# One macaron block on one core: second router's scores inside the latent attention, VectorE's output addition ahead of the row sums, the dense attention's small steps placed anew, expert lists and gathers earlier

## The chip, the core and the metric

The kernel runs on one core of one Trainium2 chip. The time is that of one launch on the device, in microseconds (us). Engines are named as in the profile: PE is TensorE's matrix multiply and PEld its weight load, DVE is VectorE, ACT is ScalarE, POOL is GpSimd, SP is SyncE, which here only issues DMAs. Lines (L554) are those of the kernel before, except where the text says that they are the changed kernel's.

## What is computed

x has 16 sequences of 512 tokens with 128 channels: 8,192 tokens, which lie as 64 tiles of 128 tokens (one batch is 4 tiles). Six residual steps follow one another, each on the layer norm of the current x:

```python
x = x + 0.5 * routed_ffn(ln(x))        # f1
x = x + latent_attention(ln(x))        # la, causal, 16 heads of 8
x = x + 0.5 * routed_ffn(ln(x))        # f2, same weights as f1
x = x + 0.5 * experts(ln(x))           # m1
x = x + cosine_attention(ln(x))        # ca ("dense"), 16 heads of 8, biases
x = x + 0.5 * experts(ln(x))           # m2
```

The routed step adds two attentions over its input. The light one works in windows of 128 tokens with 8 heads of 64. The heavy one works on 128 query and 256 key tokens per sequence, which a router picks: a score `x . routing_token` per token (one routing token for queries, one for keys), 50 steps of a coordinate descent over the 512 scores of each of 32 rows, and the largest. The expert step computes a shared feed-forward for all tokens, and routes tokens to 64 experts with a capacity of 48 rows each: their rows are gathered, multiplied and added back by scatter.

## The kernel before

`macaron_block` (L2332) runs the stages in order, each with its own arena in the on-chip memory and its own `Block`, at whose end all engines meet. x and y, the tokens before and after a stage, stay on chip. Within a block every engine has its program written out by hand, and the engines meet through counting semaphores; the order on an engine, and on SP's and POOL's DMA queues, is the order in the code.

**Router (`router_prologue`, L81).** It loads and scales the light weights (`wqkv`, `wo` in `lw`), takes the statistics of all 64 tiles (L226, DVE), and computes the scores on PE: per batch four transposes (L172), a split of the transposed tile into a bf16 part on ACT (L205) and a rest on DVE (L219), and four products (L181, L183). Then variance, square root on ACT (L209), reciprocal, a transpose of the reciprocals (L192), and scores (L254) and their maxima (L256) as 48 rows of 512. It runs twice, as f1r and f2r.

**Light attention (`light_attention`, L259).** One `body` per window of 128 tokens, 64 windows. In one window DVE takes the maxima of the logits (L534), subtracts them (L538), makes a step of the descent (`settle` L528, `descend` L522 and L523), sums the probabilities that ACT made (L546), takes the reciprocal (L550), adds the output of window i-3 to x (L554) and normalises the next tile (`make_xr`, L513). POOL multiplies the probabilities by the reciprocals (L371, two operations a window). PE's transpose of the next tile (L425) and the output of L407 share the PSUM tile `ps_a`, so PE waits at L425 for L554, and DVE waits at L513 for L425. The descent ends after window 27; from 28 on DVE carries the search for the largest scores instead, and ACT makes the next tile.

**Latent and dense attention (`stacked_attention`, L997).** Both treat 16 batches; one batch is 4 quads. The latent one has 10 units in a quad, the dense one 4 units of 4 heads in each, 16 places in a batch. The logits are computed twice from operands in bf16 parts: once for the maxima (L1302, then DVE L1721 or L1719), once with the maxima subtracted (L1313, then ACT's exponential L1575). The maxima go through a split in two bf16 parts (`mparts`), a transpose (L1382), a copy (L1742) and four small DMAs into the operand (`m_rows`, L1171). Queries and keys of a later batch are split by POOL into parts (L1187 to L1199), stored to HBM (L1151) and loaded as stacks (L1163), all on SP's queue. In the latent attention POOL also masks probabilities (L1202) and splits the maxima (L1210, L1212); in the dense one DVE splits them (`split`, L1730 and L1732). The output (L1413) is added to y by DVE: one addition in the latent attention (L1761), bias and then y in the dense one (L1763, L1765), and there `tile_stats` (L976) takes the statistics for the next stage.

**Experts (`moe_block`, L1852).** For each batch k, PE and ACT compute the shared part, POOL adds x to it (L2045) and SP stores it (L1998). After the last of these stores SP writes the list of expert tokens (L2000) and reads it back to all partitions (L2002), and POOL, after the last addition, issues the first six gathers (L2030). Then gathers, the experts' products (from L2142) and scatters (L2062) follow in a chain.

## Time and profile before

| | us |
|---|---|
| median of 3 runs (lowest to highest) | 3302.72 (3302.44 to 3307.93) |
| the profiled execution's own time | 3303.23 |
| its span | 3301.5 |
| PE busy | 2797.7 (85%) |
| DVE busy | 2312.4 (70%) |
| ACT busy | 1849.4 (56%) |
| POOL busy | 1476.8 (45%) |

| stage, by the instructions' names | from, us | to, us |
|---|---|---|
| router and light attention of f1 | 0 | 530 |
| heavy attention of f1 | 530 | 785 |
| latent attention | 785 | 1544.7 |
| router of f2 | 1544.7 | 1590.6 |
| light attention of f2 | 1590.6 | 2095 |
| heavy attention of f2 | 2095 | 2350 |
| experts m1 | 2350 | 2600 |
| dense attention | 2600 | 3062 |
| experts m2 | 3062 | 3301.5 |

The stages follow one another with a meeting of all engines between them, so what a stage gains or loses goes into the span one for one. The busy shares are averages over stages of different kinds. The profile's chain that ended last reaches back only through m2 (DMA 3%, PE 3% of the span), so each stage is read from its own stretch of the timeline and of the waits.

### The profile page before, as it was taken

The page shows a single profiled execution, that of the slowest core. Times are in us where ns is not written, and L with a number is a line of the kernel's source. Part 1 is how long each engine was busy: PE and PEld are TensorE (multiplying, and loading weights), DVE is VectorE, ACT ScalarE, POOL GpSimd, SP SyncE. Part 2 cuts the span into 40 slices and gives each one's busy share as a digit, 9 for nine tenths or more (in the row PEclk, how much of TensorE's full clock was granted, in tenths as well). Part 3 has the DMA queues.
Part 4 walks back from the last instruction along what each step waited for, and adds up shares of the span by engine and source line. Part 5 has one row for each costly group of instructions (what it writes and reads, how often), then busy time and mean ns, then how long its engine had stood idle before and what let it go on. Part 6 is the DMA issues. An engine that isn't in the chain of part 4 may idle for free. (4 is left out here: it accounts for less than half of the span.)

```text
span 3301.5 us, 72698 instructions
## 1 busy us (share of the span) xinstructions
PE 2797.7 (85%) x24552; PEld 1869.8 (57%) x24552; DVE 2312.4 (70%) x6126; ACT 1849.4 (56%) x3771; POOL 1476.8 (45%) x1662
## 2 busy tenths in 40 slices
PE   7999998997699999998888999799785278887774
PEld 4777886775233333333567777677663145555642
DVE  5887776884588888883677777599662267786641
ACT  3777664553166666664577666455541257776421
POOL 1222236883455555542122223578555354451445
PEclk9999998998599999998999999899895579999775
DMA  2000000001333333320000000000162255553532
GB/s 80 1 0 1 0 0 1 0 0 31 77 78 79 79 79 81 87 68 14 14 0 0 1 0 0 1 0 0 50 164 35 82 138 124 135 127 88 142 86 31
DMA packets 158029, 162.92 MB, mean 49 GB/s; under 512 B 43264, under 2 KB 136064, under 8 KB 157056
## 3 DMA queue, kind: packets, MB, share of 16 engines
q1 hardware_dynamic: 148032, 148.24, 17.5%
q0 software_dynamic: 9216, 7.87, 1.8%
q10 hardware_dynamic: 576, 4.19, 0.3%
q8 instruction: 114, 1.87, 0.2%
q14 instruction: 91, 0.75, 0.1%
HBM read 84.57 MB, written 74.60 MB: 48 GB/s over the span
## 5 line engine op out<-in xcount | busy, mean ns | idle before, releaser
L1721 DVE CUSTOM_DVE_ANT_0 la_ps<-la_ps,la_tri 128x512 f32<-128x512 f32 (+3 forms) x1024 | 480.4, 514 | 91.9 <-PE la_ps L1302 84.2
L1575 ACT ACTIVATE la_prob<-la_ps 128x512 f32<-128x512 f32 x640 | 374.0, 601 | 236.0 <-PE la_ps L1313 229.1
L371 POOL TENSOR_TENSOR f2l_prob<-f2l_prob,f2l_rec 128x512 f32<-128x512 f32 x128 | 132.2, 1054 | 364.2 <-DVE f2l_rec L550 364.2
L1202 POOL TENSOR_SCALAR_AFFINE_SELECT la_prob<-la_prob 128x512 f32<-128x512 f32 x256 | 159.4, 635 | 298.9 <-ACT la_prob L1575 298.7
L1302 PE MATMUL la_ps<-la_ks,la_qs 48*128 48x512 bf16 (+3 forms) x1024 | 255.3, 318 | 42.2 <-DVE la_mx L1721 26.9
L371 POOL TENSOR_TENSOR f1l_prob<-f1l_prob,f1l_rec 128x512 f32<-128x512 f32 x128 | 133.9, 1067 | 334.2 <-DVE f1l_rec L550 334.2
L1313 PE MATMUL la_ps<-la_qs,la_ks 50*128 50x512 bf16 (+3 forms) x1024 | 243.0, 311 | 4.4 <-ACT la_prob L1575 1.8
L1313 PEld LDWEIGHTS la_ps<-la_qs,la_ks 50*128 50x128 bf16 x1024 | 67.2, 94 | 234.3 <-ACT la_prob L1575 170.8
L1345 PE MATMUL la_ps_o<-la_prob,la_v 128*32 128x512 f32 (+3 forms) x2048 | 196.0, 456 | 0.0
L1719 DVE TENSOR_REDUCE ca_mx<-ca_ps 128x4 f32<-128x512 f32 x256 | 163.7, 680 | 39.8 <-PE ca_ps L1302 39.5
L1575 ACT ACTIVATE ca_prob<-ca_ps 128x512 f32<-128x512 f32 x256 | 140.4, 598 | 38.1 <-PE ca_ps L1313 36.2
L1721 DVE DVE_READ_ACCUMULATOR2_ANT la_mx<- 128x1 f32 x1024 | 142.8, 139 | 0.0
L400 PE MATMUL f1l_ps_qk<-f1l_xrT,f_wqkv 128*128 128x128 f32 x1024 | 134.5, 286 | 0.7 <-ACT f1l_xrT L496 0.7
L400 PE MATMUL f2l_ps_qk<-f2l_xrT,f_wqkv 128*128 128x128 f32 x1024 | 134.1, 285 | 0.7 <-ACT f2l_xrT L496 0.7
L1302 PEld LDWEIGHTS la_ps<-la_ks,la_qs 48*128 48x128 bf16 x1024 | 67.0, 95 | 110.6 <-DVE la_mx L1721 89.9
L400 PEld LDWEIGHTS f1l_ps_qk<-f1l_xrT,f_wqkv 128*128 128x128 f32 x1024 | 122.1, 195 | 11.7 <-issue 10.4
L400 PEld LDWEIGHTS f2l_ps_qk<-f2l_xrT,f_wqkv 128*128 128x128 f32 x1024 | 121.8, 195 | 11.8 <-issue 10.6
L1313 PE MATMUL ca_ps<-ca_qs,ca_ks 58*128 58x128 bf16 x1024 | 91.9, 224 | 41.2 <-DMA ca_ks<-stack_image 15.3
L1313 PEld LDWEIGHTS ca_ps<-ca_qs,ca_ks 58*128 58x128 bf16 x1024 | 61.1, 97 | 103.1 <-issue 60.7
L1187 POOL TENSOR_TENSOR ca_rr<-ca_qb,ca_t 128x512 f32<-128x512 f32 x32 | 44.1, 1379 | 164.9 <-ACT ca_t L1644 164.9
L546 DVE TENSOR_REDUCE f2l_rsum<-f2l_prob 128x8 f32<-128x1024 f32 x64 | 78.1, 1220 | 55.8 <-ACT f2l_prob L479 55.8
L546 DVE TENSOR_REDUCE f1l_rsum<-f1l_prob 128x8 f32<-128x1024 f32 x64 | 78.1, 1220 | 54.5 <-ACT f1l_prob L479 54.5
(551 smaller groups left out, 7979.2 us busy)
## 6 DMA issues: line engine op xcount, KB each, us to landing
stack_image<-la_parts SPq DMA_DIRECT2D x192, 128.0 KB, 2.4
stack_image<-ca_parts SPq DMA_DIRECT2D x192, 128.0 KB, 2.3
la_qs<-stack_image SPq DMA_DIRECT2D x64, 192.0 KB, 3.5
la_ks<-stack_image SPq DMA_DIRECT2D x64, 192.0 KB, 4.4
ca_qs<-stack_image SPq DMA_DIRECT2D x64, 192.0 KB, 3.8
ca_ks<-stack_image SPq DMA_DIRECT2D x64, 192.0 KB, 4.8
gather_table<-m_xn SPq DMA_DIRECT2D x32, 256.0 KB, 2.3
gather_table<-m_pr SPq DMA_DIRECT2D x32, 128.0 KB, 2.3
```

The lines of the kernel that those rows point to most:

```text
L371: nc.gpsimd.tensor_tensor(pr[:, g], pr[:, g], rc[:, g].rearrange("p (h o) -> p h o", o=1).broadcast_to([P, PAIRS, P]), ALU.mult).then_inc( ...
L400: last = nc.tensor.matmul(ps_qk[:, t, p], wqkv[:, t, p * P:(p + 1) * P], xrT[:], start=True, stop=True)
L546: nc.vector.tensor_reduce(rsum[:], prob[(u - 1) % 2][:], X_AX, ALU.add).then_inc(sum_ready, 1)
L1187: nc.gpsimd.tensor_tensor(rr[:], left[:], right[:], op)
L1202: return nc.gpsimd.affine_select(view, view, pattern=[[0, 4], [1, P]], compare_op=ALU.is_ge, fill=0.0, base=0, channel_multiplier=-1)
L1302: last = nc.tensor.matmul(bank[:, col:col + width], qs[u][rows, h // 2, qblk * P:(qblk + 1) * P], ks[u][rows, h // 2, keys], start=True, s ...
L1313: last = nc.tensor.matmul(bank[:, col:col + width], ks[u][rows, h // 2, blk * P:(blk + 1) * P], qs[u][rows, h // 2, blk * P:blk * P + widt ...
L1345: last = nc.tensor.matmul(ps_o[32 * j:32 * j + 32, blk * P:T], v[u][:, blk, 4 * q + j, :], prob[q % 2][:, unit, col:col + width], start=bl ...
L1575: nc.scalar.activation(prob[q % 2][:, n], ps2[n % 2][:], ACT.Exp, scale=SM).then_inc(S["p_sb"], 1)
L1719: last = nc.vector.tensor_reduce(m, bank[:].rearrange("p (a b) -> p a b", a=TPB), X_AX, ALU.max)
L1721: last = nc.vector.tensor_tensor_reduce(bank[:, col:col + width], bank[:, col:col + width], tri[:, T - width:T], 1.0, -BIG, ALU.add, ALU.m ...
```

## The change

1. **Router of f2.** Its 64 tiles' scores and statistics are computed while the latent attention runs. POOL multiplies the finished tiles of batch i-2 with the two centred routing tokens and adds the products up in halves (`route_dots`, three parts between the masks of quad 1); those of the last batch follow after its output. DVE takes the four statistics of batch i-1 among the maxima of quad 3. A short `router_end` takes the place of `router_prologue` for f2. The light weights stay on chip from f1.
2. **Light attention, f1 and f2.** L554, the addition of the output of window i-3, moves ahead of the wait for ACT's probabilities.
3. **Dense attention.** The small steps of a batch are placed at 16 places instead of 8 slots, on PE, DVE and ACT. POOL splits the maxima (casts before L1730 on DVE) and adds the output bias to y; DVE adds the output once. SP stores the first half of batch i+3's parts (t = 0) one body earlier and loads the first half of the stacks before the rows of maxima.
4. **Experts, m1 and m2.** The token list is stored before the output of k = 12 and read back before that of k = 13, and POOL issues the first six gathers in pairs after its additions k = 13, 14 and 15.

The heavy attention and the router of f1 are as before.

```diff
@@ router_end, vector
+            ch.step(nc.vector.tensor_tensor(diff[:], col(1), col(4), ALU.subtract))
+            nc.vector.tensor_tensor(ssq[:], col(2), col(5), ALU.add)
+            ch.step(nc.vector.tensor_tensor(diff[:], diff[:], diff[:], ALU.mult))
+            nc.vector.scalar_tensor_tensor(ssq[:], diff[:], C / 4.0, ssq[:], ALU.mult, ALU.add).then_inc(ssq_ready, 1)
+            dve.wait_ge(ssq_ready, 1)
+            nc.vector.tensor_scalar(var[:], ssq[:], 1.0 / C, LN_EPS, ALU.mult, ALU.add).then_inc(var_ready, 1)
...
+            dve.wait_ge(std_ready, 1)
+            nc.vector.reciprocal(rstd[:], std[:]).then_inc(rstd_ready, 1)
...
+            nc.vector.tensor_tensor(wide[:, :, 0:B], by_batch(dots[:, 0]), by_batch(rstd[:]), ALU.mult)
+            nc.vector.tensor_tensor(wide[:, :, KV0:KV0 + B], by_batch(dots[:, 1]), by_batch(rstd[:]), ALU.mult).then_inc(wide_ready, 1)
...
+            dve.wait_ge(r_ps, 1)
+            nc.vector.tensor_copy(s_rows[:], ps_r[:]).then_inc(rows_ready, 1)
+            nc.vector.tensor_reduce(smax[:], ps_r[:], X_AX, ALU.max)
@@ light_attention, vector, body
+                if live(i, 3):
+                    dve.wait_ge(f_ps, i - 2)
+                    j = i - 3
+                    nc.vector.scalar_tensor_tensor(
+                        y[:, bass.ds(j, 1), :].rearrange("p o c -> p (o c)"), ps_a[:, 2], 0.5,
+                        x[:, bass.ds(j, 1), :].rearrange("p o c -> p (o c)"), ALU.mult, ALU.add).then_inc(y_ready, 1)
                 if live(i, 1):
                     dve.wait_ge(p_sb, i)
                     nc.vector.tensor_reduce(rsum[:], prob[(u - 1) % 2][:], X_AX, ALU.add).then_inc(sum_ready, 1)
@@ stacked_attention, gpsimd
+            def route_dots(b, part):
...
+                    for r in range(2):
+                        last = nc.gpsimd.tensor_tensor(prod[:, r], ys, rtok[:, r:r + 1].broadcast_to([P, TPB, C]), ALU.mult)
...
+                for k, half in ((1, 64), (2, 32)) if part == 1 else ((3, 16), (4, 8), (5, 4), (6, 2), (7, 1)):
...
+                    nc.gpsimd.tensor_tensor(to, low, high, ALU.add).then_inc(S["dot_step"], 1)
             def body(i, u):
+                if not latent:
+                    if live(i):
+                        split_maxima(i, 1)
+                    if live(i, -2):
+                        split(i + 2, 1, 2, 5)
+                    if live(i, -1):
+                        split_maxima(i + 1, 0)
+                    if live(i):
+                        add_bias(i)
+                    if live(i, -3):
+                        split(i + 3, 0, 0, 5)
+                        split(i + 3, 1, 0, 2)
+                    return
...
+                if i == B:
+                    for part in range(3):
+                        route_dots(B - 1, part)
@@ stacked_attention, vector, between
+                if live(i, 1) and q == 3 and n in STATS_AT:
+                    dve.wait_ge(S["out_done"], i)
+                    nc.vector.nop(nofuse=True)
+                    j = TPB * (i - 1) + STATS_AT[n]
+                    nc.vector.bn_stats(stats[:, j], y[:, j])
@@ moe_block, sync
+                if k == LISTED - 1:
+                    sp.wait_ge(S["left_ready"], 1)
+                    sp.dma_start(lists.rearrange("(e s) -> e s", e=E), left[:].rearrange("e a s -> e (a s)")).then_inc(S["lists_stored"], 16)
+                if k == LISTED:
+                    sp.wait_ge(S["lists_stored"], 16)
+                    sp.dma_start(tb, lists.rearrange("(a s) -> a s", a=1).broadcast_to([P, E * CAP])).then_inc(S["tb_in"], 16)
```

DVE, light attention of f2, the descent, first before, then changed (`g_x` is the stage's output, `g_y` its input, `f2l_xr` the next tile normalised):

```order
L523 TENSOR_SCALAR f2l_tmin<-f_s_rows,f_na 48x512
L545 ISA
L546 TENSOR_REDUCE f2l_rsum<-f2l_prob 128x8
L547 ISA
L549 ISA
L550 RECIPROCAL f2l_rec<-f2l_rsum 128x8
L552 ISA
L554 ISA x2
L554 SCALAR_TENSOR_TENSOR g_x<-f2l_ps_a,g_y 128x128
L558 ISA
L513 ISA x2
L513 REGISTER_ALU
```

```order
L590 TENSOR_SCALAR f2l_tmin<-f_s_rows,f_na 48x512
L612 ISA
L614 ISA x2
L614 SCALAR_TENSOR_TENSOR g_x<-f2l_ps_a,g_y 128x128
L618 ISA
L619 TENSOR_REDUCE f2l_rsum<-f2l_prob 128x8
L620 ISA
L622 ISA
L623 RECIPROCAL f2l_rec<-f2l_rsum 128x8
L625 ISA
L580 ISA x2
L580 REGISTER_ALU
```

The addition (L554, now L614) stands ahead of the row sums, and the normalising of the next tile (L513, now L580) directly behind the reciprocal.

POOL, latent attention, quads 1 and 2 of a batch of the changed kernel (L1286 is the mask, `la_prod` the products, `fw_dots` the finished sums, L1295 and L1298 the split of the maxima):

```order
L1286 AFFINE_SELECT la_prob<-la_prob 128x4x128 x2
L1334 TENSOR_TENSOR la_prod<-g_y,la_rtok 128x512 x2
L1286 AFFINE_SELECT la_prob<-la_prob 128x4x128 x2
L1344 TENSOR_TENSOR la_prod<-la_prod 128x8x64
L1344 TENSOR_TENSOR la_prod<-la_prod 128x8x32
L1286 AFFINE_SELECT la_prob<-la_prob 128x4x128
L1344 TENSOR_TENSOR la_prod<-la_prod 128x8x16
L1344 TENSOR_TENSOR la_prod<-la_prod 128x8x8
L1344 TENSOR_TENSOR la_prod<-la_prod 128x8x4
L1344 TENSOR_TENSOR la_prod<-la_prod 128x8x2
L1344 TENSOR_TENSOR fw_dots<-la_prod 128x2x4
L1295 CAST la_mparts<-la_mx 128x32
```

Nine operations of the router stand between the masks and ahead of the split of the maxima; before, the masks and the split stood alone there.

POOL, dense attention, one batch of the changed kernel (`g_y` with `ca_bo` is the bias), in which the two splits of the maxima and the bias stand among the splits of queries and keys that were alone on POOL before:

```order
L1278 TENSOR_TENSOR ca_r<-ca_rr,ca_parts 128x512
L1280 TENSOR_TENSOR ca_parts<-ca_rr,ca_parts 128x512
L1283 TENSOR_TENSOR ca_parts<-ca_r,ca_parts 128x512
L1295 CAST ca_mparts<-ca_mx 128x32
L1298 TENSOR_TENSOR ca_mparts<-ca_mx,ca_mparts 128x32
L1321 TENSOR_TENSOR g_y<-g_y,ca_bo 128x512
L1271 TENSOR_TENSOR ca_rr<-ca_qb,ca_t_0 128x512
L1275 TENSOR_TENSOR ca_parts<-ca_qb,ca_t_0 128x512
L1278 TENSOR_TENSOR ca_r<-ca_rr,ca_parts 128x512
L1280 TENSOR_TENSOR ca_parts<-ca_rr,ca_parts 128x512
L1283 TENSOR_TENSOR ca_parts<-ca_r,ca_parts 128x512
```

The rest of the batch (the operations for the keys and the other split) repeats this pattern; the split of the maxima waits for the maxima that it reads, and what stands behind it waits too.

## Rows read from the trace of the kernel before

**Rows 1.** Windows, dense attention: us; busy PE, PEld, DVE, ACT, POOL; clock; DMA share; GB/s
```profile
2720.00:2960.00 240.00, 198.50 (x2938) 134.94 (x2936) 186.44 (x378) 174.02 (x331) 117.83 (x96) 0.98 0.52 131
```

**Rows 2.** Timeline (start us, us, instruction, idle before), latent attention to second light attention
```profile
1543.05 0.69 DVE L1761 TENSOR_TENSOR g_y<-la_ps_c,g_y 128x512 f32<-128x512 f32 x1 [2.58 <-PE la_ps_c L1413]
...
1581.65 0.26 DVE L232 TENSOR_TENSOR f2r_total<-f2r_st 128x64 f32<-128x64 f32 x1
...
1583.55 0.58 ACT L207 COPY f2r_dots<-f2r_ps_d 48x512 f32<-48x512 f32 x1 [2.54 <-PE f2r_ps_d L183]
1584.15 1.28 ACT L209 ACT_TABLE_LOAD   x1
...
1588.81 0.68 DVE L256 TENSOR_REDUCE f_smax<-f_s_rows 48x1 f32<-48x512 f32 x1
...
1590.62 0.35 DVE L513 SCALAR_TENSOR_TENSOR f2l_xr<-g_y,g_a,g_b 128x128 f32<-128x128 f32 x1 [1.13 <-PEq L51]
```

**Rows 3.** The timeline of one latent batch: POOL, then the matmul that reads masked probabilities
```profile
1284.95 1.22 POOL L1202 TENSOR_SCALAR_AFFINE_SELECT la_prob<-la_prob 128x512 f32<-128x512 f32 x2 [3.46 <-ACT la_prob L1575]
...
1288.11 0.25 POOL L1212 TENSOR_TENSOR la_mparts<-la_mx,la_mparts 128x32 bf16<-128x32 f32 x1
...
1296.18 1.16 POOL L1194 TENSOR_TENSOR la_r<-la_rr,la_parts 128x512 f32<-128x512 f32 x1
...
1289.11 1.07 PE L1345 MATMUL la_ps_o<-la_prob,la_v 128*32 128x512 f32 x8
```

**Rows 4.** Windows of one latent batch, and the old router's statistics by source line
```profile
1295.20:1334.50 39.30, 38.05 (x310) 13.88 (x306) 35.41 (x144) 27.42 (x52) 22.44 (x31) 1.00 0.34 83
...
L226 DVE BATCH_NORM_STATS2 f2r_st<-g_y x64: 274/277/294, 1544.8 to 1577.8; 128x6 f32<-128x128 f32 x64
```

**Rows 5.** L538, once per window: first light attention early, late; second early, late
```profile
L538 DVE TENSOR_TENSOR f1l_ssub<-f1l_ps_s,f1l_mx x25: 1223/1224/1226, 106.2 to 288.8; 128x1024 f32<-128x1024 f32 x25
...
L538 DVE TENSOR_TENSOR f1l_ssub<-f1l_ps_s,f1l_mx x31: 1223/1224/1225, 302.9 to 517.0; 128x1024 f32<-128x1024 f32 x31
...
L538 DVE TENSOR_TENSOR f2l_ssub<-f2l_ps_s,f2l_mx x24: 1223/1224/1225, 1644.6 to 1837.8; 128x1024 f32<-128x1024 f32 x24
...
L538 DVE TENSOR_TENSOR f2l_ssub<-f2l_ps_s,f2l_mx x32: 1223/1224/1226, 1853.2 to 2081.8; 128x1024 f32<-128x1024 f32 x32
```

**Rows 6.** The timeline of one window of each light attention
```profile
201.88 2.08 POOL L371 TENSOR_TENSOR f1l_prob<-f1l_prob,f1l_rec 128x512 f32<-128x512 f32 x2 [5.51 <-DVE f1l_rec L550]
...
202.69 0.38 DVE L513 SCALAR_TENSOR_TENSOR f1l_xr<-g_x,g_a,g_b 128x128 f32 x1 [0.63 <-PE f1l_ps_a L425]
...
1708.05 2.04 POOL L371 TENSOR_TENSOR f2l_prob<-f2l_prob,f2l_rec 128x512 f32<-128x512 f32 x2 [6.43 <-DVE f2l_rec L550]
...
1708.49 0.33 PE L425 MATMUL f2l_ps_a<-g_ident,f2l_xr 128*128 128x128 f32 x1 [1.19 <-DVE g_x L554]
...
1709.20 1.03 DVE L513 SCALAR_TENSOR_TENSOR f2l_xr<-g_y,g_a,g_b 128x128 f32 x1 [0.77 <-PE f2l_ps_a L425]
```

**Rows 7.** Waits of PE, dense attention, 2720 to 2960: us, times, longest
```profile
PE ca_ps L1313 <- DMA ca_ks<-stack_image: 12.5, 10, 3.0
...
PE ca_ps_a L1354 <- DVE ca_mT L1742: 4.8, 9, 0.5
PE ca_ps L1302 <- DVE ca_mx L1719: 4.2, 9, 0.7
...
PE ca_ps_a L1382 <- DVE ca_mparts L1732: 3.7, 11, 0.3
```

**Rows 8.** L1763, once per batch of the dense attention
```profile
L1763 DVE TENSOR_TENSOR ca_added<-ca_ps_c,ca_bo x13: 690/691/692, 2717.0 to 3009.9; 128x512 f32<-128x512 f32 x13
```

**Rows 9.** The timeline before the first experts: an output addition, the third gather, its first use
```profile
2460.59 1.27 POOL L2045 TENSOR_TENSOR m_ob<-m_ob,g_x 128x512 f32<-128x512 f32 x1 [2.24 <-ACT m_ob L2214]
...
2470.08 0.95 POOL L2030 DMA_INDIRECT m_xs<-gather_table,m_gidx  x1 [0.30 <-issue]
...
2477.13 0.87 PE L2142 MATMUL m_ps_t<-g_ident,m_xs 128*128 128x128 f32 x3 [11.96 <-DMA m_xs<-gather_table,m_gidx]
```

More of the change, by code:

```diff
@@ L1406, in turn_y @@
                 pe.wait_ge(S["yt_ready"], 4 * b + 4)
+                if not latent and live(b, -2):
+                    pe.wait_ge(S["mT_sb"], 2 * b + 5)
                 for j in range(TPB):
@@ L1418, in between @@
                 if not latent:
[L1419 to L1420 removed]
+                    place(i, u, q, n)
                     return
@@ new lines, in place @@
+                    for part in range(2):
+                        project_out(part)
+                if k == 13 and live(i, -4):
+                    xn_t(i + 4)
+                if n == 2:
+                    b, qb = (i, q - 2) if q >= 2 else (i - 1, q + 2)
+                    if live(i, 0 if q >= 2 else 1):
+                        otr(b, qb)
+                if n >= 2:
+                    b, qb, ub = (i, q - 1, u) if q else (i - 1, 3, 1 - u)
+                    if live(i, 0 if q else 1):
+                        pv(b, ub, qb, (0, 1) if n == 2 else (2, 3))
@@ L1533, in xn_t @@
+                if k == 15 and live(i, -2):
+                    if live(i, -3):
+                        pe.wait_ge(S["floored"], 2 * i + 8)
+                    if live(i, 1):
+                        pe.wait_ge(S["out_done"], i)
+                    for part in range(2):
+                        project_v(i + 2, u, part)
             def xn_t(b):
@@ L1661, in _ @@
             make_xn(0)
-            if not latent:
-                xnT_copy(0, 0)
             batches(act, body)
@@ L1709, in maxima @@
             def maxima(b, q, n):
-                if latent and n == 0 and q % 2 == 0 and past(b, 1):
+                if n == 0 and q % 2 == 0 and past(b, 1):
                     dve.wait_ge(S["m_ready"], 2 * b - 1 + q // 2)
@@ L1876, in moe_block @@
         w2 = A.sb("w2", [P, EP, C])
-        xn = [A.sb(f"xn{u}", [P, TPB, C]) for u in range(XR)]
+        xn = [A.sb(f"xn{u}", [P, TPB, C]) if free is None else free[:, u].rearrange("p (j c) -> p j c", j=TPB) for u in range(XR)]
         score = A.sb("score", [P, NT, E])
```

433 lines of the change are left out of this document (244 added, 189 removed).

## The prediction

> **What bounds the kernel now.** The stages meet one after another, so I read the busy engines by stage first, then the timeline of the two or three repeated pieces, then the waits. No one engine bounds the whole. In the latent attention PE works 38.05 of 39.30 us of a batch and DVE 35.41 [rows 4]: whatever is added to either shows. Between latent attention and the second light attention there is a bare seam: from the end of the last output (1543.05 + 0.69 = 1543.74) to the first tile of the next stage (1590.62) pass 46.9 us [rows 2]. The light attention goes round a loop through DVE: sum, reciprocal, addition, PE's transpose, next tile, maxima. In the dense attention PE is busy 198.5 of 240 us [rows 1], and its idle time is a collection of small waits [rows 7].
>
> **1. Router of f2.** The old stage goes. In its place stand: (a) POOL's products and sums of batch 15, which follow the last output. A POOL operation on 128x512 takes 1.16 us [rows 3], so two products and the first halving cost about 3.5 us. The next four halvings lie between 1.16 us and the 0.25 us of a 128x32 operation [rows 3]; on the line through these two they cost about 0.67, 0.43, 0.31 and 0.25 us. Two more at about 0.25 us and some 0.1 us between dependent ones give 6.3 us. (b) The meeting of the engines, 1.1 us, as at the end of the old router (1589.49 to 1590.62). (c) `router_end`: before, from the copy of the scores (1583.55) to the end of the row maxima (1588.81 + 0.68 = 1589.49) were 5.9 us [rows 2]. Of these go the copy (0.58) and the table load (1.28), which nothing holds back now. About five small DVE operations of 0.26 us, which had been hidden, come in: 5.3 us. (d) The second meeting, 1.1 us. Sum 13.8 us against 46.9: **33 us saved**, between 28 (every small POOL operation at 0.6 us, the table load exposed) and 36.
>
> **2. What it costs inside the latent attention.** DVE gets four statistics per batch; one takes 0.28 us [rows 4], so 1.1 us. DVE has 3.9 us free in a batch, PE 1.25, and in quads 2 and 3 each waits for the other now and then, so I charge half of it, 0.55 us a batch over 15 batches: **8 us lost**. The ends are 0 (all of it in DVE's own idle time) and 17 (1.1 us, all 15 on the path); I take the middle, since PE and DVE have so little to spare.
> POOL gets 6.2 us a batch and is 22.44 us busy of 39.3 [rows 4]. The two products fit the 3.46 us in which POOL waits ahead of the second pair of masks [rows 3]. The next part delays one mask by about 1 us and the last part the split of the maxima by about 3 us. The masked probabilities of the pair at 1284.95 are read by PE's product of 1289.11 [rows 3], 2.9 us after they end, so I cost this at nothing; what covers it is PE's own queue of logits, and if it is gone, each microsecond past that margin is lost in every batch.
> The row says 1.16 us for POOL's 128x512. By the Trainium skill ("GPSIMD Engine Reference", 4.1 Engine selection) elementwise work on two tensors belongs on VectorE, GpSimd being about twice as slow. By that page, as an estimate, part (a) would take half its time on VectorE, 3 us less in the seam, and each full batch would load VectorE with 3 us more.
>
> **3. Light attention.** L538 starts every (288.8 - 106.2) / 24 = 7.61 us in the first, (1837.8 - 1644.6) / 23 = 8.40 us in the second, and (2081.8 - 1853.2) / 31 = 7.37 us in the late windows of the second [rows 5]. In the second PE waits 1.19 us for the addition before its transpose, DVE then 0.77 us for the transpose, and the next tile takes 1.03 us instead of the 0.38 us of the first [rows 6], because POOL's two operations (2.04 us together) have begun at 1708.05. The change takes both waits away. The next tile is ready to start right behind the reciprocal, at about the moment at which POOL starts. If POOL is first, the tile ends some 0.1 us after POOL's first operation, at 1708.05 + 1.02 + 0.13 = 1709.2, where it now ends at 1710.23: 1.0 us less. But the following steps then fall beside POOL's second operation and lose about 0.3 us: period 7.7, 0.7 x 24 = **17 us saved**. In the first light attention the tile ends at 203.07 now, and POOL's first operation at 201.88 + 1.04 = 202.92 [rows 6]: it would end no sooner, and gains nothing. In the late windows the 7.37 fall to the (517.0 - 302.9) / 30 = 7.14 us of the late windows of the first [rows 5], the same loop with the same work, which I take for PE's own time: 0.23 x 30 = **7 us saved**. Sum **24**, ends 0 and 48 (rival B).
>
> **4. Dense attention.** A batch takes (3009.9 - 2717.0) / 12 = 24.4 us [rows 8]. In 240 us, 9.8 batches, PE waits 12.5 us for the loads of the stacks, 4.8 and 3.7 for copies and splits of the maxima and 4.2 for maxima [rows 7]: 25.2 us, 2.6 a batch. The split of the maxima goes to POOL, where its operation on 128x32 takes 0.25 us [rows 3]; the loads start before the rows of maxima instead of after. If all four waits go, the period is 21.8 us; over 12 periods **31 us saved**. PE is busy 20.3 us a batch [rows 1], so the best end is 4.1 x 12 = 49; the other end is 0, if the waits come back elsewhere. Of the new waits, POOL's split of the maxima (i+1, first half) holds back the bias and seven splits behind it. Those take about 1.2 + 7 x 1.2 = 9.6 us, and it is released in the middle of the batch: with a period of 21.8 they end about 1 us before the next body. The bias is due only at place 13 and SP's early store only in the next body, so both are costed at nothing.
>
> **5. Experts.** The first use of the gathers is at 2477.13, 7.05 us after the third gather was issued at 2470.08 [rows 9]. After k = 13's addition (2460.59 + 1.27) two gathers take 2.5 us, then k = 14's addition 1.3 us, so the third is issued at about 2465.7: 4.4 us earlier. The read of the list, which shared the DMA engines with the gathers, is earlier too, so the landing may be 2 to 3 us quicker. I take 7 us for each expert stage, **14 us saved**, ends 8 and 16.
>
> **Sum.** 3303.2 - 33 + 8 - 24 - 31 - 14 = **3209 us**. The durations come from the profiled execution, whose own time of 3303.2 is 0.5 us above the median of 3302.7. I do not correct for it.
>
> **Rivals.**
> A. **The dense attention gives nothing** (or the light one, with 24 us): the load's wait becomes a wait of the same length for the parts, since POOL's chain is in order. For it: POOL gets the splits, 1 us of slack. Against it: the load is 1.3 us late in a batch only. 3209 + 31 = 3240.
> B. **VectorE first.** The next tile starts before POOL's operation and POOL waits 0.4 us. For it: in the first light attention the tile takes only 0.38 us though it begins 0.2 us before POOL's first operation ends [rows 6]. Then both light attentions go at PE's 7.14: (7.61 - 7.14) x 24 = 11 and (7.70 - 7.14) x 24 = 13 us more, 3209 - 24 = 3185. The Trainium skill ("SBUF — State Buffer", Who interferes with whom) has it that VectorE with two inputs in SBUF and a reading GpSimd exclude each other, and the one that starts first keeps the ports for its whole instruction. The 1.03 us of the tile agree.
> C. **Latent attention dearer**: statistics and masks cost 2 us a batch instead of 0.5: 3209 + 22 = 3231.
> D. **Slower than before.** In the latent attention POOL's 6.2 us of products delay masks and maxima by their full length, and DVE's and PE's queues stand behind them. With 0.7 us for DVE operations that wait for POOL's ports and 0.6 us already charged that is 7 us a batch: 3209 + 6.9 x 15 = 3312. It is slower from 6.3 us a batch on. Against it: the masks of rows 3 end 2.9 us before they are read and POOL is idle 17 us of a batch.
>
> **Chances.** My forecast 0.50, A 0.17, B 0.18, C 0.10, D 0.03, none of these 0.02. The range goes from B with a little more from the dense attention (3209 - 24 - 19 = 3166) to A with the bounds of the latent attention (3240 + 12 = 3252). No change within 0.2% (6.6 us, about what a measurement of this kernel can tell) needs nearly all terms to fail: 0.02; slower 0.03; faster 0.95.
>
> **What would show it.** Right: the second light attention's first tile some 14 us after the last latent output; L538's period at 7.7 in the second and 7.6 in the first light attention, PE's wait for the addition gone; a latent batch like that of rows 4 at about 39.9 us; dense batches at 21.8 us with no wait of PE for the stacks; the first use of a gather 7 us earlier against the last output addition. Wrong: a period of 7.14 in the first light attention (B), PE waiting for `ca_mparts` or `ca_ks` as long as now (A), waits for `la_prob` from POOL (D).

## The result and the profile after

| | before | changed |
|---|---|---|
| median of the runs, us | 3303.18 (3302.44 to 3307.93) | 3192.97 (3186.59 to 3201.53) |
| ratio, 95% interval | | 0.9665 (0.9637 to 0.9693) |
| the profiled execution's own time | 3303.23 | 3201.53 |
| its span | 3301.5 | 3199.8 |

The forecast was 3209 us with a range of 3166 to 3252. The sum was 16 us above the median, and two of its terms were wrong by more than that in opposite directions, the latent attention by 19.5 and the light one by 17 us: that they nearly cancel is luck. The two traces say where the 101.7 us between the two spans went; each line is a difference of two instants or stretches of the traces.

| part | forecast, us | measured, us |
|---|---|---|
| seam, last latent output to first tile of f2 | -33 | -32.6 |
| latent attention, first to sixteenth output | +8 | +27.5 |
| light attention, f1 and f2 | -24 | -7.9 and -33.1 |
| dense attention | -31 | -35.5 |
| experts, from the addition of k = 13 on | -14 | -7.6 and -7.7 |
| shared part of m2 up to that addition | 0 | -5.5 |
| shared part of m1 and all other stretches | 0 | +0.7 |

The shared part of m2 has the same instructions as before; its granted clock was 0.81 before and 0.85 now.

**The seam** is as costed. The timeline of the changed kernel, beside rows 2:

```profile
1564.40 0.69 DVE L1895 TENSOR_TENSOR g_y<-la_ps_c,g_y 128x512 f32<-128x512 f32 x1 [3.50 <-PE la_ps_c L1553]
...
1565.23 2.49 POOL L1334 TENSOR_TENSOR la_prod<-g_y,la_rtok 128x512 f32<-128x512 f32 x2 [1.78 <-DVE g_y L1895]
1567.86 3.93 POOL L1344 TENSOR_TENSOR la_prod<-la_prod 128x512 f32<-128x512 f32 x6
1571.93 0.20 POOL L1344 TENSOR_TENSOR fw_dots<-la_prod 128x8 f32<-128x8 f32 x1
...
1577.93 0.67 DVE L323 TENSOR_REDUCE f_smax<-f2r_ps_r 48x1 f32<-48x512 f32 x1
...
1579.39 0.35 DVE L580 SCALAR_TENSOR_TENSOR f2l_xr<-g_y,g_a,g_b 128x128 f32<-128x128 f32 x1 [0.79 <-PEq L51]
```

From the end of the last output, 1565.09, to the first tile are 14.3 us (forecast 13.8): POOL's products and sums up to 1572.13 take 7.0 (6.3), `router_end` with its two meetings 7.3 (7.5).

**The latent attention** lost 27.5 us where 8 were forecast. The whole stretch by windows (us; busy PE, PEld, DVE, ACT, POOL; granted clock; DMA; GB/s), of the kernel before:

```profile
972.60:1543.00 570.40, 545.29 (x4311) 198.68 (x4303) 470.65 (x1913) 384.84 (x712) 291.92 (x403) 0.97 0.29 71
```

and of the changed one:

```profile
966.50:1564.40 597.90, 570.46 (x4311) 208.06 (x4303) 479.88 (x1973) 384.65 (x712) 378.77 (x538) 0.92 0.28 68
```

PE runs the same 4311 matmuls and is busy 25.2 us longer, while the granted clock fell from 0.97 to 0.92. DVE got 60 statistics and 9.2 us, POOL 87 us. So most of the loss is PE at its lower level of 1.2 GHz. The batches tell it too: they take 42.5 and 39.5 us in turn up to the ninth output. The 39.5 are near what an undisturbed batch took before (rows 4: 39.3), and the 42.5 hold a stretch of 6.8 us at half the clock, always 12 us after an output addition. That is in quad 3, where the statistics stand. The last four intervals between outputs hold 9.2 of the 27.5 us; there PE stayed at the low level for 30.7 us in one piece, where it was 17.1 us before. One place in quad 3 by PE's timeline and by windows:

```profile
978.15 0.54 PE L1431 MATMUL la_ps<-la_ks,la_qs 48*128 48x512 bf16 x1 [0.72 <-DVE la_mx L1862]
```

```profile
978.30:985.10 6.80, 6.80 (x27) 2.96 (x26) 3.43 (x12) 2.29 (x4) 3.64 (x6) 0.50 0.50 112
```

PE waits 0.72 us for a maximum of DVE, and 0.15 us after it resumes the clock is at the low level, with PE busy all the time. In a batch between, the same wait at the same place leaves the clock high:

```profile
1184.54 0.39 PE L1431 MATMUL la_ps<-la_ks,la_qs 48*128 48x512 bf16 x1 [0.72 <-DVE la_mx L1862]
```

```profile
1184.70:1191.50 6.80, 6.80 (x61) 3.09 (x62) 5.89 (x24) 3.84 (x7) 6.18 (x9) 1.00 0.45 111
```

So a wait precedes the fall, but does not decide it alone. What POOL does in the same batches is as forecast (its timeline, beside rows 3):

```profile
1280.54 2.55 POOL L1334 TENSOR_TENSOR la_prod<-g_y,la_rtok 128x512 f32<-128x512 f32 x2
1284.03 1.22 POOL L1286 TENSOR_SCALAR_AFFINE_SELECT la_prob<-la_prob 128x512 f32<-128x512 f32 x2 [0.95 <-ACT la_prob L1701]
...
1287.31 0.63 POOL L1286 TENSOR_SCALAR_AFFINE_SELECT la_prob<-la_prob 128x512 f32<-128x512 f32 x1
1287.91 1.67 POOL L1344 TENSOR_TENSOR la_prod<-la_prod 128x128 f32<-128x128 f32 x4
...
1290.51 0.25 POOL L1298 TENSOR_TENSOR la_mparts<-la_mx,la_mparts 128x32 bf16<-128x32 f32 x1 [0.43 <-ACT la_prob L1701]
```

The two products end before POOL would have had to mask (it still waits 0.95 us for ACT), and the split of the maxima comes about 3 us later in the batch than in rows 3.

**The light attention** gained 41 us. L605 is the old L538; first light attention early and late, second early and late, beside rows 5:

```profile
L605 DVE TENSOR_TENSOR f1l_ssub<-f1l_ps_s,f1l_mx x25: 1224/1225/1225, 106.0 to 289.1; 128x1024 f32<-128x1024 f32 x25
...
L605 DVE TENSOR_TENSOR f1l_ssub<-f1l_ps_s,f1l_mx x31: 1224/1224/1225, 303.1 to 509.8; 128x1024 f32<-128x1024 f32 x31
...
L605 DVE TENSOR_TENSOR f2l_ssub<-f2l_ps_s,f2l_mx x27: 1224/1225/1227, 1623.9 to 1823.7; 128x1024 f32<-128x1024 f32 x27
...
L605 DVE TENSOR_TENSOR f2l_ssub<-f2l_ps_s,f2l_mx x30: 1224/1225/1226, 1837.8 to 2037.4; 128x1024 f32<-128x1024 f32 x30
```

The descent goes at 183.1 / 24 = 7.63 us in the first and 199.8 / 26 = 7.68 in the second (forecast 7.6 and 7.7). The late windows go at 206.7 / 30 = 6.89 and 199.6 / 29 = 6.88 (forecast 7.14 in both). One descent window of each, by the timeline, beside rows 6:

```profile
202.34 2.08 POOL L438 TENSOR_TENSOR f1l_prob<-f1l_prob,f1l_rec 128x512 f32<-128x512 f32 x2 [5.65 <-DVE f1l_rec L623]
202.35 1.17 DVE L580 SCALAR_TENSOR_TENSOR f1l_xr<-g_x,g_a,g_b 128x128 f32 x1
...
1705.30 0.27 PE L492 MATMUL f2l_ps_a<-g_ident,f2l_xr 128*128 128x128 f32 x1
...
1705.90 2.08 POOL L438 TENSOR_TENSOR f2l_prob<-f2l_prob,f2l_rec 128x512 f32<-128x512 f32 x2 [5.71 <-DVE f2l_rec L623]
1706.09 0.99 DVE L580 SCALAR_TENSOR_TENSOR f2l_xr<-g_y,g_a,g_b 128x128 f32 x1 [0.27 <-issue]
...
1707.50 0.76 DVE L590 TENSOR_SCALAR f2l_tmin<-f_s_rows,f_na 48x512 f32<-48x512 f32 x1
```

PE's transpose waits for nothing. The next tile, 0.35 us alone, is now drawn out beside POOL's operation instead: it starts 0.01 us after POOL in the first and 0.19 us after it in the second, and takes 1.17 and 0.99 us, so that it ends 0.15 us behind POOL's first operation. In five windows of the first it is the tile that starts ahead, by up to 0.03 us, and it takes 1.20 to 1.22 us all the same:

```profile
179.22 1.22 DVE L580 SCALAR_TENSOR_TENSOR f1l_xr<-g_x,g_a,g_b 128x128 f32 x1
...
179.25 1.04 POOL L438 TENSOR_TENSOR f1l_prob<-f1l_prob,f1l_rec 128x512 f32<-128x512 f32 x1 [5.59 <-DVE f1l_rec L623]
```

**The dense attention** by windows and by the waits of PE, beside rows 1 and 7, and its output additions, beside rows 8:

```profile
2680.00:2920.00 240.00, 221.56 (x3336) 137.95 (x3338) 172.25 (x370) 187.31 (x358) 149.28 (x162) 0.99 0.56 145
```

```profile
PE ca_ps_b L1527 <- ACT ca_xnT L1793: 6.9, 10, 0.8
PE ca_ps_a L1483 <- ACT ca_yT L1728: 5.1, 11, 0.6
PE ca_ps_c L1613 <- DVE ca_v L1938: 2.2, 10, 0.3
```

```profile
L1895 DVE TENSOR_TENSOR g_y<-ca_ps_c,g_y x13: 680/681/693, 2659.6 to 2923.1; 128x512 f32 x10, 128x512 f32<-128x512 f32 x3
```

A batch takes 263.5 / 12 = 22.0 us (forecast 21.8), PE is busy 92% of it. The waits of rows 7 are gone but for three single ones of 1.9 us together; the three shown are new, 14.2 us in 240.

**The experts**, beside rows 9:

```profile
2415.15 1.26 POOL L2172 TENSOR_TENSOR m_ob<-m_ob,g_x 128x512 f32<-128x512 f32 x1 [2.24 <-ACT m_ob L2343]
...
2420.51 0.96 POOL L2157 DMA_INDIRECT m_xs<-gather_table,m_gidx  x1 [0.16 <-issue]
...
2424.90 0.88 PE L2271 MATMUL m_ps_t<-g_ident,m_xs 128*128 128x128 f32 x3 [5.18 <-DMA m_xs<-gather_table,m_gidx]
```

From the addition of k = 13 to the first use of the gathers 9.75 us pass, before 16.54: 6.8 less, forecast 7. To the last scatter it is 7.6 us less.

### The profile page after: what moved, and what is told of

Read it like the earlier page. It is cut to its first block and busy times, and to the rows that moved or that the text cites. A ratio compares the mean times of both kernels' runs of the same rounds, so it can differ in the third digit from the quotient of the medians.

```text
span 3199.8 us, 72888 instructions
## 1 busy us (share of the span) xinstructions
PE 2754.1 (86%) x24406; PEld 1839.3 (57%) x24406; DVE 2276.2 (71%) x6034; ACT 1825.2 (57%) x3752; POOL 1591.7 (50%) x1872
## 5 line engine op out<-in xcount | busy, mean ns | idle before, releaser
L1286 POOL TENSOR_SCALAR_AFFINE_SELECT la_prob<-la_prob 128x512 f32<-128x512 f32 x256 | 159.4, 634 | 228.9 <-ACT la_prob L1701 228.8
L1860 DVE TENSOR_REDUCE ca_mx<-ca_ps 128x4 f32<-128x512 f32 x256 | 173.6, 687 | 98.6 <-PE ca_ps L1431 97.5
L1474 PE MATMUL la_ps_o<-la_prob,la_v 128*32 128x512 f32 (+3 forms) x2048 | 207.1, 479 | 0.0
L1701 ACT ACTIVATE ca_prob<-ca_ps 128x512 f32<-128x512 f32 x256 | 152.1, 602 | 83.7 <-PE ca_ps L1442 83.7
L467 PE MATMUL f1l_ps_qk<-f1l_xrT,fw_wqkv 128*128 128x128 f32 x1024 | 133.0, 284 | 0.7 <-ACT f1l_xrT L563 0.7
L467 PE MATMUL f2l_ps_qk<-f2l_xrT,fw_wqkv 128*128 128x128 f32 x1024 | 133.0, 284 | 0.7 <-ACT f2l_xrT L563 0.7
L467 PEld LDWEIGHTS f1l_ps_qk<-f1l_xrT,fw_wqkv 128*128 128x128 f32 x1024 | 120.7, 194 | 11.7 <-issue 10.5
L467 PEld LDWEIGHTS f2l_ps_qk<-f2l_xrT,fw_wqkv 128*128 128x128 f32 x1024 | 120.7, 194 | 11.7 <-issue 10.4
L546 ACT ACTIVATE f2l_prob<-f2l_ssub 128x1024 f32<-128x1024 f32 x64 | 67.7, 1058 | 85.0 <-DVE f2l_ssub L605 82.3
L546 ACT ACTIVATE f1l_prob<-f1l_ssub 128x1024 f32<-128x1024 f32 x64 | 67.7, 1058 | 79.5 <-DVE f1l_ssub L605 79.5
L1431 PE MATMUL ca_ps<-ca_ks,ca_qs 56*128 56x128 bf16 x1024 | 97.8, 223 | 10.2 <-DMA ca_ks<-stack_image 7.2
```

What stands on the lines that cost most here:

```text
L467: last = nc.tensor.matmul(ps_qk[:, t, p], wqkv[:, t, p * P:(p + 1) * P], xrT[:], start=True, stop=True)
L546: nc.scalar.activation(prob[(u - 1) % 2][:], ssub[:], ACT.Exp, scale=SM).then_inc(p_sb, 1)
L1286: return nc.gpsimd.affine_select(view, view, pattern=[[0, 4], [1, P]], compare_op=ALU.is_ge, fill=0.0, base=0, channel_multiplier=-1)
L1431: last = nc.tensor.matmul(bank[:, col:col + width], qs[u][rows, h // 2, qblk * P:(qblk + 1) * P], ks[u][rows, h // 2, keys], start=True, s ...
L1474: last = nc.tensor.matmul(ps_o[32 * j:32 * j + 32, blk * P:T], v[u][:, blk, 4 * q + j, :], prob[q % 2][:, unit, col:col + width], start=bl ...
L1701: nc.scalar.activation(prob[q % 2][:, n], ps2[n % 2][:], ACT.Exp, scale=SM).then_inc(S["p_sb"], 1)
```

## The experiments

All twelve kernels start from the changed kernel. They ran in three series beside runs of the kernel before, whose own runs spread from 3289 to 3312 us, so the stages are compared in the traces, and times only where they were repeated. Where one trace stands for a kernel, the text says "one profile".

### Which work makes the latent attention slower

Theory S: the statistics in quad 3. Theory P: POOL's products. Each is taken out of the loop in turn and done after the last output; the statistics are also moved to quad 0.

In stats_end the statistics leave `between` and stand behind `batches(dve, body)`; in dots_end the calls of `route_dots` leave quad 1 and stand behind `batches(pool, body)`.

```diff
@@ stats_end, vector
+            if latent:
+                dve.wait_ge(S["out_done"], B)
+                nc.vector.nop(nofuse=True)
+                for j in range(NT):
+                    nc.vector.bn_stats(stats[:, j], y[:, j])
@@ dots_end, gpsimd
+            if latent:
+                for b in range(B):
+                    for part in range(3):
+                        route_dots(b, part)
@@ stats_q0, vector, between
-                if live(i, 1) and q == 3 and n in STATS_AT:
+                if (live(i, 2) and q == 0 or i == B and q == 3) and n in STATS_AT:
+                    late = 1 if q == 3 else 2
```

> The changed kernel, but the 64 statistics of the latent attention's output all follow its last output instead of standing four to a batch in quad 3. Theory S (the statistics delay the maxima in quad 3, PE waits there, and the clock falls behind it in every second batch): the low-clock stretches of 6.8 us at the same place of every second batch go, and first to last output addition of the latent attention comes back from 598 us to about 572 us, some 26 us less; the seam grows by 60 statistics of 0.22 us, 13 us. Time about 3180. Theory P (POOL's products are the cause, through masks, the split of the maxima or the shared ports): the first to last output addition stays within 4 us of 598, the seam grows by 13 us, time about 3206.

> The changed kernel, but POOL's products and sums of all 16 batches follow the last output; the seam grows by 15 times 6.3 us, 95 us. Theory P: first to last output addition of the latent attention falls from 598 to about 572 us, time about 3262. Theory S: it stays within 4 us of 598, time about 3288.

> The changed kernel, but the statistics of batch i-2 stand in quad 0 of batch i, where DVE has neither the rotations of quads 1 and 3 nor the output addition of quad 2 (those of the last batch stay in quad 3). Theory S: quad 3 no longer waits longer than before, the low-clock stretches fall to the 3.4 us ones of the kernel before or fewer, first to last output addition 575 us or less, time about 3172. Theory P: no change, 3193.

The same stretch, first to sixteenth output addition, by windows; of stats_end:

```profile
966.40:1530.20 563.80, 537.94 (x4311) 196.44 (x4303) 470.77 (x1914) 384.45 (x712) 378.69 (x538) 0.98 0.29 72
```

of dots_end:

```profile
970.60:1563.70 593.10, 565.25 (x4311) 207.00 (x4303) 479.51 (x1974) 384.58 (x712) 298.48 (x413) 0.93 0.28 69
```

of stats_q0:

```profile
966.40:1550.80 584.40, 556.71 (x4311) 203.86 (x4303) 478.62 (x1973) 385.78 (x712) 378.53 (x538) 0.94 0.28 70
```

With all of POOL's products in the loop and no statistics the stretch takes 563.8 us and its first six batches 39.3 us each; without the products and with the statistics it takes 593.1, 1 us outside the band that theory S gave. In these profiles S holds and P falls: 80 us of work on POOL cost nothing that can be seen. In quad 0 the statistics bring the clock down as well, in stretches of 3.4 us about once a batch instead of 6.8 us in every second, and the batches take 40.9 us each; there the expectation of 575 us or less missed.

How the statistics bring the clock down is shown only in part. They lengthen PE's waits, but by little: from the first to the twelfth output PE waits for maxima 12.4 us in stats_end, 13.4 in the changed kernel and 14.2 in stats_q0, while the stretch itself takes 436, 459 and 450 us. In stats_q0 no such wait is longer than 0.6 us. Why 1 to 2 us more of waits bring the clock down so much more often stays open.

The size of the loss is less fixed than its cause. With the statistics in quad 3 the stretch took 577 to 598 us in ten profiles (the changed kernel's two, 597.9 and 579.8, and those of the eight others that leave this code alone); without them in the loop it took 564 and 570, and 570 before the change in one profile. So the forecast of 8 us is met by the shortest of them, and the profiled execution shows the longest. The times: stats_end 3186.5 us (3173 to 3199), ratio 0.9654 (0.961 to 0.9699); stats_q0 3187.8, 0.9642 (0.9604 to 0.9679); both no different from the changed kernel by their intervals. The profile of stats_end is of a run of 3176.5 us, and two of its four runs took over 3196, so the whole times do not confirm the gain. dots_end 3289.4. stats_end's seam grew by 5.5 us, not by 13, since DVE's statistics run beside POOL's last products.

### The light attention

y_late puts the output addition of the search windows behind the reciprocal again (`if live(i, 3) and late(i, r):`), and leaves the descent as changed.

> The changed kernel, but in the windows of the search (28 and later) VectorE's output addition stands behind the reciprocal again, as before the change; the descent windows keep the new order. Theory D (in these windows the loop goes through VectorE, and the addition now lies in its wait for ACT's probabilities): the late period goes back from 6.89 us to about 7.15 us in the first and 7.4 us in the second light attention, so 8 and 16 us more, while PE's own time is below 6.9. Rival (PE's wait at its transpose for the addition is all of it): 7.15 in the second as in the first, since in the first PE waited only 2.2 us in 23 windows; the first stays below 7.0.

The time of the one run was 3206.6 us; its latent attention happened to be 21 us shorter than in the changed kernel's profile, so only the stages are compared. L605 of y_late, late windows of the first and of the second light attention:

```profile
L605 DVE TENSOR_TENSOR f1l_ssub<-f1l_ps_s,f1l_mx x31: 1223/1224/1225, 304.6 to 518.7; 128x1024 f32<-128x1024 f32 x31
...
L605 DVE TENSOR_TENSOR f2l_ssub<-f2l_ps_s,f2l_mx x28: 1223/1224/1225, 1849.0 to 2046.7; 128x1024 f32<-128x1024 f32 x28
```

214.1 / 30 = 7.14 and 197.7 / 27 = 7.32 us: the old periods are back, in the first as in the second. The two stages are 9.8 and 14.6 us longer than in the changed kernel. So the loop goes through DVE, and 7.14 us was never PE's own time. The waits say why; in the first light attention, 320 to 480, of the kernel before:

```profile
DVE f1l_rsum L546 <- ACT f1l_prob L479: 27.7, 23, 1.2
...
PE f1l_ps_a L425 <- DVE g_y L554: 2.2, 6, 1.0
```

and of the changed kernel:

```profile
DVE g_y L614 <- PE f1l_ps_a L474: 25.3, 22, 1.2
```

Before, DVE stood idle 1.2 us a window until ACT's probabilities came, and did the addition after them. Now the addition stands in that time, and DVE hardly waits for ACT.

xr_first moves the next tile ahead of the reciprocal in the descent:

```diff
                     nc.vector.tensor_reduce(rsum[:], prob[(u - 1) % 2][:], X_AX, ALU.add).then_inc(sum_ready, 1)
+                if live(i, -2) and not late(i, r):
+                    dve.wait_ge(xrT_ps, i + 2)
+                    make_xr(i + 2)
+                if live(i, 1):
                     dve.wait_ge(sum_ready, i)
...
-                if live(i, -2) and not late(i, r):
-                    dve.wait_ge(xrT_ps, i + 2)
-                    make_xr(i + 2)
```

> The changed kernel, but in the descent windows of both light attentions DVE normalises the next tile between the row sums and the reciprocal, so before POOL's operations can start. Theory (the tile takes 1.0 to 1.2 us behind the reciprocal only because POOL's first operation has the ports, and this lies in DVE's loop): the tile takes 0.38 us, POOL starts about 0.3 us later, the descent period falls from 7.7 and 7.8 us to about 7.0 in both, 24 windows each: about 34 us less, time 3160. Rival (another loop, PE with ACT, sets the period, or POOL's later start does): 7.5 us or more, time 3185 to 3200.

One window of its second light attention, by the timeline:

```profile
1677.03 0.35 DVE L580 SCALAR_TENSOR_TENSOR f2l_xr<-g_y,g_a,g_b 128x128 f32 x1 [0.39 <-PE f2l_ps_a L492]
...
1677.97 0.92 DVE L590 TENSOR_SCALAR f2l_tmin<-f_s_rows,f_na 48x512 f32<-48x512 f32 x1
```

The tile takes 0.35 us, as expected, but the descent period falls only from 7.63 and 7.68 to 7.41 and 7.53 us, between theory and rival: the tile, which now starts 0.54 us ahead of POOL in nearly every window, waits up to 0.4 us for PE's transpose, and the stall beside POOL is passed on to `f2l_tmin`, 0.92 us instead of 0.76 (0.47 in the median). The two stages are 6.5 and 5.6 us shorter. Its time is 3184.5 us, 0.9643 (0.9619 to 0.9667).

### The dense attention

Four edits were undone, each alone but for the bias, and then all four, so that only the 16 places stay. split_dve puts the split of the maxima back on DVE, behind places 7 and 15; rows_first sends the rows of maxima ahead of the first load; store_late stores both halves of a batch's parts together; place_only does all of this and adds the bias on DVE in a second operation again.

```diff
@@ rows_first, sync, body
-                if latent and live(i, -1):
+                if live(i, -1):
                     m_rows(i + 1, 1 - u, 0)
@@ store_late, sync, body
-                    if latent:
-                        store_parts(i + 2, u, 0)
+                    store_parts(i + 2, u, 0)
...
-                if not latent and live(i, -3):
-                    store_parts(i + 3, 1 - u, 0)
@@ split_dve, vector, place
+                if k in (7, 15) and live(i, -1):
+                    split(i + 1, k // 8)
```

> The changed kernel, but in the dense attention VectorE splits the maxima again (behind places 7 and 15) and POOL does not. Theory (the cast waits for POOL's ports, 1.1 us instead of 0.2, and PE's transpose and the maxima wait behind it): cast 0.7 to 1.2 us, dense batch 22.0 us to about 22.8 us, dense stage 8 to 12 us longer. Rival (the placement at 16 places and the loads gave it all): batch within 0.2 us of 22.0.

> The changed kernel, but in the dense attention SP sends the rows of maxima of the next batch before it loads the first half of the stacks, as before the change. Theory (the 1.3 us a batch that PE waited for the stacks came from SP's order): PE waits for the loads of the stacks again, about 1.2 us a batch, batch 23.2 us, stage 15 us longer. Rival (the early store of the first parts and the shorter batch leave slack): no wait, batch within 0.2 us of 22.0.

> The changed kernel, but in the dense attention SP stores both halves of a batch's parts together before its loads, as before the change. Theory (the early store takes 3.8 us of SP's queue off the way to the loads, and this ended PE's wait for the stacks): PE waits for the stacks again about 1 us a batch, batch 22.0 to 23 us or more. Rival (the places alone): batch within 0.2 us of 22.0.

> The changed kernel with the four other edits of the dense attention undone together: rows of maxima first, both halves stored together, the split of the maxima and the bias on VectorE. Only the 16 places stay. Theory (the places give most of it): batch 22.0 to 22.8 us against 24.4 before. Rival (the edits cover for one another, each alone being undone without loss): batch 23.5 us or more, with PE waiting for the stacks and for the split.

| one profile each | batch, us | stage, us | whole time, us |
|---|---|---|---|
| kernel before | 24.4 | 467.3 | 3303.2 |
| changed | 22.0 | 431.8 | 3201.5 |
| changed_again | 22.1 | 439.6 | 3187.8 |
| split_dve | 22.0 | 436.3 | 3194.2 |
| rows_first | 21.9 | 433.5 | 3195.7 |
| store_late | 21.9 | 443.0 | 3210.8 |
| place_only | 25.2 | 481.1 | 3233.6 |

The batch is a mean over twelve intervals. The twelfth differs (19.5 to 22.3 us among these four and split_dve); over the first eleven the changed kernel, changed_again, rows_first and store_late all take 22.1 us, and split_dve 22.2. So each of the three alone can be undone at a loss of 0.2 us a batch at most, and all three single theories fell. In split_dve the median of the casts, 0.18 us, says little: of the two casts of a batch one takes 0.18 us, at a place where POOL is idle, and the other, up to the twelfth batch, 0.86 to 1.10 us beside POOL's splits, as was expected of all:

```profile
2712.97 1.15 POOL L1280 TENSOR_TENSOR ca_parts<-ca_rr,ca_parts 128x512 bf16<-128x512 f32 x1
2713.31 0.86 DVE L1867 CAST ca_mparts<-ca_mx 128x32 bf16<-128x32 f32 x1
```

PE waits for the split 0.9 us a batch there, and makes most of it up elsewhere. With all undone, the batch is longer than before the change. The waits of place_only, 2700 to 2920, and its additions of y:

```profile
PE ca_ps_a L1510 <- DVE ca_mparts L1863: 11.5, 9, 2.2
...
PE ca_ps L1432 <- DMA ca_ks<-stack_image: 0.7, 2, 0.4
```

```profile
L1894 DVE TENSOR_TENSOR g_y<-ca_added,g_y x13: 691/1518/1749, 2646.0 to 2948.7; 128x512 f32 x10, 128x512 f32<-128x512 f32 x3
```

PE waits 1.3 us a batch for the split, and the addition of y, two inputs on chip while POOL works, takes 1.52 us in the median where the changed kernel's takes 0.68. The granted clock is 0.93 from 2700 to 2920, against 0.99 in the changed kernel, so part of the 3.2 us is the clock's. Three batches of place_only at the full clock, and four of the kernel before, by windows:

```profile
2852.00:2923.60 71.60, 62.08 (x922) 38.11 (x918) 56.49 (x117) 51.91 (x98) 33.51 (x28) 1.00 0.49 126
```

```profile
2868.10:2965.00 96.90, 80.86 (x1224) 54.93 (x1224) 77.07 (x156) 71.92 (x137) 49.41 (x41) 1.00 0.52 131
```

That is 23.9 and 24.2 us a batch, where the changed kernel takes 22.1: at an equal clock the places alone are worth 0.3 us, the other four edits 1.8, and the rest of the 3.2 is the clock. PE hardly waits for the stacks (0.7 us), though the loads stand in their old order: with the places, and in this longer batch, that wait is gone without the other edits. Either the four edits cover for one another, or the bias, which no run undid alone, carries the 1.8 us by itself: both fit. Which pair does it was not tried either.

### The experts

moe_list_late stores and reads the token list after the last output, as before, and leaves the gathers early.

> The changed kernel, but in both expert stages the token list is stored and read back after the last output, as before the change, while the gathers stay early. From the last but two output addition (k = 13) to the first scatter the change took 6.8 us off. Theory (4.4 us from the earlier issue, the rest from the read of the list no longer sharing the DMA engines): the first use of a gather comes within 1 us of the changed kernel's, since the list now comes after it, but the first scatter waits for the list and is back within 1.5 us of the kernel before, so about 6 us more in each expert stage. Rival (only the gathers matter): the first scatter stays within 1 us of the changed kernel's.

```profile
2399.16 1.27 POOL L2170 TENSOR_TENSOR m_ob<-m_ob,g_x 128x512 f32<-128x512 f32 x1 [2.24 <-ACT m_ob L2341]
...
2424.51 1.62 POOL L2189 DMA_INDIRECT x_after_experts<-m_yc,m_sidx  x1 [14.12 <-DVE m_sidx L2432]
```

From the addition to the first scatter it is 25.3 us (25.7 in m2); the changed kernel has 19.9, the one before 26.7. The first use of a gather stays at 9.6 us. So the gathers' earlier issue is worth little by itself: without the earlier list only 1.4 us of 6.8 are left, as the theory had it. The opposite, the list early and the gathers late, was not run, so what the list is worth alone is not shown. The time of the one run was 3202.5 us.

### A version that is better than both

changed_again is the changed kernel once more. In `both`, the next tile comes first as in xr_first, and the statistics of batches 0 to 14 stand in the last body of the latent attention, where DVE has no maxima:

```diff
-                if live(i, 1) and q == 3 and n in STATS_AT:
+                if i == B and q < 3:
+                    dve.wait_ge(S["out_done"], B - 1)
+                    nc.vector.nop(nofuse=True)
+                    for j in range(2 * (UQ * q + n), 2 * (UQ * q + n) + 2):
+                        nc.vector.bn_stats(stats[:, j], y[:, j])
+                if i == B and q == 3 and n in STATS_AT:
```

> The changed kernel as it is, on the chip and beside the runs of the two that follow, since its runs differed by 15 us: ratio to the kernel before 0.964 to 0.969, about 3187 to 3200 us.

> The changed kernel with two edits: VectorE normalises the next tile before the reciprocal (12 us less in the two light attentions, as xr_first showed), and the statistics of batches 0 to 14 stand in the last body of the latent attention (batch 16, two at each of 30 places), where VectorE has no maxima to take. Theory S: the first to last output addition of the latent attention takes 564 to 572 us instead of 577 to 598, and the seam stays at 14.9 us; time 3155 to 3165, ratio to the kernel before about 0.957. Rival (the statistics delay the last outputs, or the clock falls anyway): the last batch's 18 to 22 us become 28 or more, time 3175 or more.

changed_again: 3191.96 us (3179.65 to 3205.69, 6 runs), 0.9668 (0.9644 to 0.9691). `both`: 3167.57 us (3165.35 to 3174.56, 5 runs), 0.9597 (0.9582 to 0.9612), 24 us less, the intervals apart. Of the 22.4 us between the spans of the two profiles, 10.7 stand in the light attentions and 9.3 in the latent stretch:

```profile
962.10:1532.60 570.50, 541.37 (x4311) 197.49 (x4303) 481.15 (x1968) 384.62 (x712) 378.65 (x538) 0.97 0.28 71
```

Its first six batches take 39.3 us and from the last output's start to the next stage are 15.0 us, as in the changed kernel, but the last output came 21.4 us after the one before, 3.5 more than in stats_end: 28 of the statistics ran in a row up to that addition. The time lies 3 us above the range that was expected.

## Why the prediction was right, and where it was not

1. **The seam (33 us): right**, 32.6 measured.
2. **The latent attention (8 us lost): mis-sized.** The cause was the one named (the statistics beside the maxima), the step that failed is "I charge half of it, 0.55 us a batch". It priced DVE's microseconds and not the clock. An undisturbed batch lost only 0.2 us, and most of what was lost came in the low-clock stretches: by the mean clock, (1 - 0.92) x 2 x 598 = 96 us of the stretch at the low level, against (1 - 0.97) x 2 x 570 = 34 before; in stats_end, without the statistics in the loop, the stretch took 563.8 us, 34 less than in the changed kernel's profile. Over the profiles the loss is 7 to 27 us. POOL's part, costed at nothing, cost nothing that can be seen, and with it fell rival D; rival C had the size, with masks that had no part in it.
3. **The light attention (24 us): 41 measured.** The descent was right in both (0 and 17). The late windows failed at "which I take for PE's own time": the period of 7.14 was DVE's loop, of which the moved addition was a part, so that the first light attention gained 8 us, and the second 15 instead of 7. The trace had it: in the late windows of the first, PE hardly waits for the addition (2.2 us in 23 windows), and from this I took it that nothing was to be gained there. But an instruction can lengthen the loop of its own engine without another engine waiting for it, and here DVE waited 1.2 us a window for ACT ahead of it. y_late settles it.
4. **The dense attention (31 us): right in size**, 35.5 with its ends, 22.0 against 21.8 us a batch; in changed_again the stage is 8 us longer, at a lower clock. Rival A fell. The reason was not shown right: the four waits went, but neither POOL's split of the maxima, nor the order of the loads, nor the early store, to which I gave them, carries it alone, and the bias was not tried alone.
5. **The experts (14 us): right**, 15.3 measured. The early list, which I had costed only as a transfer out of the gathers' way, is needed for most of it (5.4 us of 6.8 to the first scatter).
6. Rival B, VectorE first, did not come: behind the reciprocal the tile starts within 0.03 us of POOL in most windows of the first light attention, and is drawn out in all of these. By the Trainium skill ("SBUF — State Buffer", Who interferes with whom) the one that starts first keeps the ports which the two engines share. The trace agrees where the distance is clear: 0.19 us behind POOL the tile took 0.99 us, and 0.54 us ahead of it, in xr_first, 0.35. The five windows in which it took 1.20 us or more with a start of up to 0.03 us ahead do not fit by the recorded starts, so the profile does not tell who was first there. With the tile ahead, xr_first brought 12 us and not 24, since a later operation of DVE (`f2l_tmin`) was then drawn out instead.

## What to carry to other kernels

Where two engines are both nearly full, price added work by the clock it may bring down, not by its own microseconds: 9 us of statistics cost 7 to 27, and 80 us on an engine with slack cost nothing that could be seen. A period that two stages share is not the floor of an engine; look whether the moved instruction lies in the loop of its own engine before taking its wait for all there is. When several edits go in together, undo each singly and all at once, and compare at an equal clock: here each of three looked worthless alone, and all four together were worth 1.8 us a batch, 3.2 with the clock; the fourth, left out of the single runs, leaves the question open.

## What the runs showed of the hardware

- In the latent attention of the changed kernel the granted clock of PE fell to its lower level (0.50) for 6.8 us, 0.15 us after PE resumed from a wait of 0.72 us, with PE busy 6.80 of these 6.80 us. The same wait of 0.72 us in a batch between left it at 1.00, and in stats_q0 it fell for 3.4 us behind waits of 0.58 us. So the length of the last wait does not tell when it falls; what does, no run here shows.
- The same kernel's latent stretch took 580 and 598 us in two executions, with a mean clock of 0.96 and 0.92. The spread of the changed kernel's runs, 3180 to 3206, is of that size.
- An operation of VectorE of 0.35 us that starts 0.01 us after one of GpSimd took 1.17 us. When it was moved 0.54 us ahead, it took 0.35, and a later operation of VectorE (`tmin`, 0.47 us in the median) took 0.92.
